# Which PSUM banks the attention phase of an eight-core transformer-layer kernel uses

## The reference

```python
qk_in = xb @ proj_qk_w.T + proj_qk_b
v_in  = xb @ proj_v_w.T + proj_v_b
q = qk_in @ wq.T + bq ; k = qk_in @ wk.T + bk ; v = v_in @ wv.T + bv   # 8 heads of 128
scores = einsum('nqhd,nkhd->nhqk', q * scale, k); scores[diagonal] = min
o = einsum('nhqk,nkhd->nqhd', softmax(scores), v)
x = layernorm(x + (o @ out_proj_w.T + out_proj_b))
x = layernorm(x + moe(x))      # gate, top 2 of 8 experts, silu(x W1) * (x W2) W3
```

## Time and profile before

| | us |
|---|---|
| runs (three) | 8030.1, 8039.57, 9201.7 |
| median | 8039.57 |
| profiled execution, whole | 8032.52 |
| its span on the slowest core (core 5) | 8030.6 |
| span of the other cores | 7995.3 to 8029.2 |
| TensorE busy (matmul), core 5 | 6349.5 (79%) |
| VectorE busy, core 5 | 2023.1 (25%) |
| ScalarE busy, core 5 | 1149.8 (14%) |

### The profile page before, as it was taken

The page is one execution under the profiler, slowest core; times in us unless marked ns, Lnnn a source line. Parts: engine busy times, 40 slices in busy tenths (PEclk is TensorE's granted clock), DMA queues, the critical chain, the costliest instruction groups (busy, mean ns, idle before and its releaser), DMA issues.

```text
span 8030.6 us, 77072 instructions; the slowest of 8 cores (7995.3 to 8030.6 us)
## 1 busy us (share of the span) xinstructions
PE 6349.5 (79%) x29024; PEld 2822.5 (35%) x29024; DVE 2023.1 (25%) x3464; ACT 1149.8 (14%) x1845; POOL 316.3 (4%) x599
## 2 busy tenths in 40 slices
PE   4544455551999999949999994899999949999995
PEld 1211122220344444414444442344444414444442
DVE  1344433333222222222222222222222222222222
ACT  1111111120111111121111111111111121111111
POOL 0000000000000000000000000000000000000000
PEclk9766777775999999969999997899999969999997
DMA  4111000103244433333433433234343333433431
GB/s 77 32 32 32 20 25 25 25 27 66 42 84 78 76 74 69 77 86 64 75 68 67 91 74 92 45 75 84 74 77 71 76 84 69 74 69 63 90 74 55
DMA packets 145302, 512.76 MB, mean 64 GB/s; under 512 B 45693, under 2 KB 45822, under 8 KB 135978
## 3 DMA queue, kind: packets, MB, share of 16 engines
q0 software_dynamic: 88304, 423.82, 28.8%
q1 hardware_dynamic: 56634, 84.02, 3.3%
HBM read 889.49 MB, written 41.94 MB: 116 GB/s over the span
## 4 chain that ended last, share of the span: by engine, by line
PE 75%; DVE 11%; DMA 5%; issue 3%; ACT 3%; another core or an unknown queue 1%; DVEq 1%; SPq 0%; ACTq 0%; POOLq 0%
PE pm L846 23%; PE pm L781 21%; PE pm L806 20%; PE pb L381 4%; PE pb L339 3%; DMA w1f<-w1T 3%; DVE ob L477 2%; PE pb L520 2%; DMA x1g<-x1f 2%; DVE Pb L417 1%; DVE Sb L424 1%; DVE ob L474 1%; DVE hsb L816 1%; DVEq L117 1%
## 5 line engine op out<-in xcount | busy, mean ns | idle before, releaser
L781 PE MATMUL pm<-x1T,w1f 128*128 128x512 bf16 x8192 | 1863.2, 381 | 28.9 <-DMA w1f<-w1T 24.6
L846 PE MATMUL pm<-w3sb,hsb 128*128 128x512 bf16 x8192 | 1814.8, 385 | 64.9 <-DVE hsb L816 62.2
L806 PE MATMUL pm<-x1T,w2f 128*128 128x512 bf16 x8192 | 1851.6, 379 | 0.0
L816 DVE SCALAR_TENSOR_TENSOR hsb<-pm,b2c_s,su 128x512 bf16<-128x512 f32 x1024 | 768.7, 751 | 2824.5 <-PE pm L781 2495.8
L792 ACT ACTIVATE su<-pm,b1c_s 128x512 bf16<-128x512 f32 x1024 | 703.6, 687 | 4581.2 <-PE pm L781 4463.7
L846 PEld LDWEIGHTS pm<-w3sb,hsb 128*128 128x128 bf16 x8192 | 809.7, 99 | 1071.7 <-issue 136.5
L781 PEld LDWEIGHTS pm<-x1T,w1f 128*128 128x128 bf16 x8192 | 800.6, 98 | 1014.6 <-issue 67.6
L806 PEld LDWEIGHTS pm<-x1T,w2f 128*128 128x128 bf16 x8192 | 801.5, 98 | 966.8 <-issue 0.6
L859 DVE SCALAR_TENSOR_TENSOR acc<-pm,comb,acc 128x512 f32<-128x512 f32 x512 | 384.5, 751 | 1468.9 <-PE pm L846 1454.7
L494 PE MATMUL trb<-idnb_s,obf 128*128 128x128 bf16 x256 | 32.4, 306 | 631.8 <-DVE obf L485 631.8
L678 PE MATMUL pm<-wgT_s_s,x1T 128*128 128x8 bf16 x256 | 11.3, 167 | 435.7 <-DVE gout L685 382.1
(11 more groups left out here) (94 smaller groups left out, 1921.9 us busy)
## 6 DMA issues: line engine op xcount, KB each, us to landing
w1f<-w1T POOLq DMA_DIRECT2D x256, 512.0 KB, 5.2
w2f<-w2T POOLq DMA_DIRECT2D x256, 512.0 KB, 7.3
w3sb<-w3T POOLq DMA_DIRECT2D x64, 2048.0 KB, 22.7
xres<-x SPq DMA_DIRECT2D x32, 512.0 KB, 4.5
x1f<-ob SPq DMA_DIRECT2D x32, 512.0 KB, 3.1
x1g<-x1f SPq DMA_DIRECT2D x32, 512.0 KB, 4.2
out<-outg SPq DMA_DIRECT2D x32, 512.0 KB, 2.9
Xbf<-x POOLq DMA_DIRECT2D x8, 1024.0 KB, 9.5
```

The costliest lines, as they stand in the source:

```text
L781: return t.matmul(gb[:, :], w1f[sl % 2][:, kt * 256 + off: kt * 256 + off + 128], x1T[:, kt * MCH + half * 512: kt * MCH + half * 512 + 51 ...
L806: return t.matmul(vb[:, :], w2f[sl % 2][:, kt * 256 + off: kt * 256 + off + 128], x1T[:, kt * MCH + half * 512: kt * MCH + half * 512 + 51 ...
L816: return v.scalar_tensor_tensor(hsb[:, f * MCH + half * 512: f * MCH + half * 512 + 512], vb[:, :], b2c[:, e * 16 + f: e * 16 + f + 1], su ...
L846: return t.matmul(bk[:, :], hsb[:, f * MCH + j * 128: f * MCH + j * 128 + 128], w3sb[:, f * D + half * 512: f * D + half * 512 + 512], sta ...
```

## The change

Only the choice of PSUM banks in phase A changes; no instruction is added or removed, and no engine's order changes.

- The input transposes (step 2) all go to `tr0`, where they alternated between `tr0` and `tr1`.
- The products (step 4): q uses banks (2, 3), k (4, 5) and v (2, 3), where they used (0, 1), (2, 3) and (4, 5). `proj_fm` keeps banks 0 and 1.
- The transposes of `obf` and of `x1bf` (step 6) all go to `tr1`, where they alternated.
- The output projection uses banks 4 and 5 instead of 0 and 1.

```diff
-            bk = trb[i % 2]
-            bname = f"tr{i % 2}"
+            bk = trb[0]
+            bname = "tr0"
             bankdeps = [t_xl] + take(bname) + (CONST if c == 0 and i == 0 else [])
@@
-                ("q", qk_in, wqT, bq_r, aw[2], qk_ev, (0, 1)),
-                ("k", qk_in, wkT, bk_r, aw[3], qk_ev, (2, 3)),
-                ("v", v_in, wvT, bv_r, aw[4], v_ev, (4, 5)),
+                ("q", qk_in, wqT, bq_r, aw[2], qk_ev, (2, 3)),
+                ("k", qk_in, wkT, bk_r, aw[3], qk_ev, (4, 5)),
+                ("v", v_in, wvT, bv_r, aw[4], v_ev, (2, 3)),
@@
-            bname = f"tr{par}"
-            bk = trb[par]
+            bname = "tr1"
+            bk = trb[1]
             tdeps = [t_obf] + take(bname)
@@
-                bname2 = f"pb{half}"
-                bk2 = pband[half]
+                bname2 = f"pb{4 + half}"
+                bk2 = pband[4 + half]
                 mmdeps = [t_oT, aw[5]] + take(bname2)
@@
-            bname3 = f"tr{(i + 1) % 2}"
-            bk3 = trb[(i + 1) % 2]
+            bname3 = "tr1"
+            bk3 = trb[1]
             tdeps = [t_x1bf] + take(bname3)
```

## The result

The changed kernel is slower by half a per cent: the ratio of its time to that of the kernel before is 1.0055, with a 95% interval of 1.0037 to 1.0073. Timed a second time, beside the kernel before on the same chip, it came out at 1.0051 (1.0028 to 1.0073). Its undisturbed executions take 8076.2, 8076.2 and 8080.3 us; the profiled one is the last of these, 8080.34 us, with a span of 8078.5 against 8030.6 before. The median of all eight executions is 8874.71 us, because in five of them the cores of one die or of both ran at a lower clock, which happens to the kernel before too (its median over ten is 8260.02); all that follows compares undisturbed executions, or undisturbed cores.

What follows compares the result with a forecast made beforehand. TensorE was busy 79% of the span; in phase A, roughly the first quarter, engines take turns, so chunk-start delays count fully. Terms 34.6 - 9.1 + 28.3 - 8.2 = +45.6 us gave a forecast of 8082, range 8058 to 8112.

Steps and rivals of the forecast that it cites:

- part 1: Products: the next tile's q waits for ScalarE's copy of V, 1.44 us at 24 places, +34.6 us.
- part 2: First q group of each chunk no longer waits for the v_in copy, 1.14 us earlier eight times, -9.1 us.
- part 3: Input transposes on one bank: each group waits for the previous copy, 3.54 us more eight times, +28.3 us.
- part 4: Next chunk's input transposes need not wait for VectorE's x1bf copy, 1.17 us earlier seven times, -8.2 us.
- part 5: Step 6, transposes of obf and x1bf and output projection: sharing banks costs nothing; 32 us if wrong.
- part 6: TensorE's clock, at its rise in the first projection and at the products' holes: taken as 0, bounds -15.4 to +8.0 us.
- phase B: The part after phase A, untouched by the change: predicted to last as long as before.
- Rival 1: Chunk start: clock rises sooner as transposes begin earlier and last longer, up to 15.4 us back, 8067; chance 0.07.
- Rival 4: Products: VectorE, not K, sets their end, so part 1 vanishes, 8047; chance 0.04.
- Rivals 2 and 3: Products: clock falls briefly after each hole, +40, 8122, chance 0.06; or stays low throughout, 8445, chance 0.03.

Runs made afterwards that it cites:

- gains only: Against the kernel before: q on banks 2,3, k on 4,5, v on 0,1, step 6 as in the change, input transposes still alternating; ratio 0.9981.
- pairs in turn: Against the changed kernel: product groups take banks (2,3) and (4,5) in turn over all twelve groups; ratio 1.0023 to the kernel before.
- early order with the changed banks: Changed kernel, but next chunk's input transposes and projections issued during VectorE's scores, softmax and first weighted sum; ratio 0.9768 to the kernel before.

## Why the prediction was right or wrong

| term | predicted | measured |
|---|---|---|
| part 1, v and q share a pair | +34.6 | 24 starts later by 1.43, +34.3 |
| part 2, q leaves the projection's banks | -9.1 | 14.96 to 13.81 in chunk 1, 1.15 x 8 = -9.2 |
| part 3, one bank for input transposes | +28.3 | 5.78 to 9.38 in chunk 1, 3.60 x 8 = +28.8 |
| part 4, no wait for L591 | -8.2 | 2.02 to 0.80 in chunk 1, 1.22 x 7 = -8.5 |
| part 5, step 6 | 0 | waits at L494 and L585 the same within 0.1 |
| part 6, clock | 0 (-15 to +8) | +2.6 in the `qk_in` projections, +1.1 in VectorE's wait for the output projections (192.1 against 191.0) |
| sum, phase A | +45.6 | +49.1 from these terms, +48.8 by the span |
| phase B | 0 | -0.2 |

**Right: the mechanism and its sum.** All four terms on the path came out within 0.5 us of their prediction. The experiments that split the change show parts 3 and 4 each by itself and parts 1 and 2 together, where the waits tell them apart: 24 for `V` are there, none for `v_in` is. What carried the prediction was the question asked of the earlier trace rows: which k group does VectorE wait for, and which hand-overs lie ahead of it. The forecast of 8082 lies 2 to 6 us above the undisturbed executions of the first timing, and within those of the second (8074.9 to 8086.3).

**Wrong: the spread of the executions.** The median over all executions, 8874.71, is far outside the range of 8058 to 8112. The step that failed is the sentence that begins "Its own spread is the runs' (8030 to 8040)". It takes two of the three times shown and drops the third, 9201.7, without a reason from the profile, and no rival and no part of the chances stands for an execution like it. The runs showed in its place that such executions are no exception: about half of those of the kernel before, and five of the eight that make the median of the changed one, the slowest at 9195.69. The range holds for undisturbed executions; for a plain median it needed a second part that reached up to 9200.

One of the profiles caught a disturbed execution (8437.16 us, the kernel with the gains only). Its cores 6 and 7 have a granted clock of 0.81 in the dense stretches of their first 2.9 ms, where sixteen matmuls of the products take 4.38 instead of 3.62, and about 1.00 in those after it. Cores 4 and 5 have about 1.00 in dense stretches until 5.6 ms and 0.81 in those of their last 2.8 ms. The cores of the other die have no such stretch. The two stretches are about equally long, as if the two pairs of cores had started 5.6 ms apart and the clock was lower while all four worked. The traces do not say when one core starts against another, so this is a guess, and what brings the disturbance on stays open.

**Mis-sized: the clock at a chunk's start (part 6).** I left it at 0. It measured +2.6: the projections to `qk_in` take 129.8 in total against 127.2. The groups of the changed kernel in phase A, by line:

```profile
L339 PE MATMUL pb<-xT,qkwT_s 128*128 128x512 bf16 x512 | 129.8, 421 | 10.7 <-ACT xT L319 10.7
L339 PE MATMUL pb<-xT,vwT_s 128*128 128x512 bf16 x512 | 111.8, 379 | 0.0
```

It is not the single bank alone that does this. Over the cores with all matmuls recorded:

| kernel, old order of work | `qkwT` in total, us |
|---|---|
| before | 127.1 to 127.5 |
| only the products changed | 125.0 to 127.0 |
| only the input transposes on one bank | 125.7 to 127.7 |
| only step 6, so the transposes start sooner | 126.9 to 129.2 |
| both (changed kernel, two profiles) | 129.1 to 130.0 |
| both, every group on one pair | 129.1 to 131.0 |
| both, pairs in turn | 128.8 to 130.2 |
| gains only: start sooner, alternate (undisturbed die) | 124.6 to 126.2 |

The loss of some 2.5 us comes where the transposes start sooner and share one bank, which is about what the parts by themselves do not add up to (2.4). Why is not shown. Rival 1, that the clock would rise sooner because the transposes start sooner and last longer, went the other way.

**Right by luck: no fall of the clock at the holes.** The argument was that a hole of 2.21 us in phase B left the clock alone and one of 3.59 did not, hence 1.4 is on the safe side. The changed kernel bears out the result. The kernel with every group on one pair breaks the argument: there the clock fell behind holes of 1.48 and 1.65, barely longer than the changed kernel's 1.37. The length of a hole does not decide alone, since 2.21 was harmless in phase B and 1.65 in chunk 1 of that same kernel; what else decides was not tried. One hole that was survived is no bound for holes in another place. The price taken from the 3.59 us hole, 1.68, was exact (1.69 measured).

Rival 4, covered holes, is excluded by the kernel that changes the products alone. Rivals 2 and 3 are excluded for the changed kernel by the times of its groups.

## What to carry to other kernels

Reusing a buffer costs time only where no other work stands between its last reader and its next writer, and only on the chain. Between v and the next q nothing stands, and each hand-over costs 1.44 us; with one group in between it costs nothing, even with fewer banks than the kernel before had. So rotate over the banks in the order of issue, not by the name of the product. And if TensorE idles for 40 us in every chunk while another engine works, the order of the work is worth more than any choice of banks: 3.1% here against 0.2%.

## What the runs showed of the hardware that I had not expected

- TensorE's granted clock fell to the lower level behind holes of 1.48 and 1.65 us, the first ones after the unbroken projections of chunks 0 and 2, although a hole of 2.21 us in phase B and one of 1.65 us at the end of chunk 1 had left it at 1.00. A fall cost 1.69 us and came two or three times per core among 88 holes.
- When the next chunk's transposes follow directly on a dense stretch, the first groups run at the full clock (sixteen in 1.07) and the next already at the low one (sixteen in 2.13), behind a hole of 1.48; with single-bank transposes the hole there is 1.93. The projection behind them starts at the low clock and takes about 15.6 instead of 13.98.
- In the profiled execution of the early order with the changed banks, the first early projection of 64 matmuls took 17.31 us on core 5 and 15.56 on core 1, and the next one 16.98 against 13.98. From 201 to 222 us the granted clock of cores 4 and 5 was 0.81, where cores 0, 1, 2 and 7 had 1.00, and it was 0.81 again in parts of their next 350 us. That is the level of the disturbed execution, on two cores only and for a short time. What brought it on stays open.
